# Two banks for x1, a rewritten first chunk border, and x turned into three banks

## The reference

```python
e = stack([tbl_f[ids[:, f]] for f in range(39)], axis=1)      # (512, 39, 16)
x1 = einsum('bid,bjd,ijh->bhd', e, e, W0.reshape(39, 39, 128))
x2 = einsum('bid,bjd,ijh->bhd', e, x1, W1.reshape(39, 128, 128))
z = sum(concatenate([x1, x2], axis=1), axis=-1)               # (512, 256)
h = concatenate([z, dense_ctx], axis=1)
h = maximum(h @ W_top1 + b_top1, 0)                           # 512
h = maximum(h @ W_top2 + b_top2, 0)                           # 256
y = h @ W_top3                                                # (512, 1)
```

## Time and profile before

| what | value |
|---|---|
| median of three runs | 247.56 us (246.15 to 249.37) |
| profiled execution | 246.15 us, span 244.3 us |
| granted TensorE clock, mean | 0.978 of full |
| TensorE matmul busy | 218.0 us (89%) |
| VectorE busy | 160.3 us (66%) |
| ScalarE busy | 156.5 us (64%) |
| GpSimd busy | 119.0 us (49%) |

### The profile page before, as it was taken

The page is one execution under the profiler, slowest core; times in us unless marked ns, Lnnn a source line. Parts: engine busy times, 40 slices in busy tenths (PEclk is TensorE's granted clock), DMA queues, the critical chain, the costliest instruction groups (busy, mean ns, idle before and its releaser), DMA issues.

```text
span 244.3 us, 4536 instructions
## 1 busy us (share of the span) xinstructions
PE 218.0 (89%) x1601; PEld 170.7 (70%) x1601; DVE 160.3 (66%) x325; ACT 156.5 (64%) x300; POOL 119.0 (49%) x119
## 2 busy tenths in 40 slices
PE   4587997999298999979999999998899999999896
PEld 4487565676165677867678588886586788887895
DVE  3988899699339894567686775584868664743101
ACT  3986887779368756466856857577757755653101
POOL 4787788777877877787877878400000000000000
PEclk9959999999979999999999999999999999999999
DMA  5970089030000000000000000000000000000000
GB/s 142 246 251 16 11 241 276 12 91 5 5 7 9 7 10 6 7 7 8 7 7 10 7 7 9 5 0 3 0 0 4 1 0 3 0 0 3 0 3 0
DMA packets 8362, 8.72 MB, mean 36 GB/s; under 512 B 3095, under 2 KB 5948, under 8 KB 8340
## 3 DMA queue, kind: packets, MB, share of 16 engines
q1 hardware_dynamic: 4660, 7.48, 10.8%
q0 software_dynamic: 3680, 0.95, 3.6%
HBM read 8.42 MB, written 0.00 MB: 34 GB/s over the span
## 4 chain that ended last, share of the span: by engine, by line
PE 44%; POOL 32%; issue 14%; ACT 7%; DMA 2%; DVE 1%; ACTq 0%; DVEq 0%
POOL emb L392 32%; PE turn_bank L496 12%; PE x_bank L435 5%; PE pair_bank L417 5%; PE x_bank L438 4%; PE x_bank L437 4%; PE g_bank L474 4%; PE turn_bank L534 3%; PE turn_bank L507 2%; ACT prod_hi L946 2%; PE x_turn_bank L452 2%; ACT prod L941 1%; ACT x1h L958 1%; DMA emb<-tbl,ids_sb 1%; DMA ids_sb<-ids 1%
## 5 line engine op out<-in xcount | busy, mean ns | idle before, releaser
L392 POOL DMA_INDIRECT emb<-tbl,ids_sb x115 | 118.8, 1033 | 37.3 <-issue 34.8
L941 ACT ACTIVATE prod<-pair_bank 128x512 f32<-128x512 f32 (+1 forms) x112 | 65.8, 600 | 46.8 <-PE pair_bank L417 42.0
L435 PE MATMUL x_bank<-prod_hi,pair_w_hi 128*128 128x512 f32 (+1 forms) x112 | 62.5, 558 | 7.4 <-ACT x1h L958 5.9
L787 DVE TENSOR_TENSOR prod_lo<-prod,prod_hi 128x512 fp32r<-128x512 f32 x96 | 64.8, 685 | 2.3
L417 PE MATMUL pair_bank<-x,sel 117*128 117x512 bf16 (+1 forms) x112 | 42.6, 384 | 2.2 <-ACT prod L941 1.5
L496 PE MATMUL turn_bank<-g_sb,w_sb 128*128 128x128 f32 x312 | 42.7, 279 | 0.6 <-ACT g_sb L968 0.6
L496 PEld LDWEIGHTS turn_bank<-g_sb,w_sb 128*128 128x128 f32 x312 | 39.4, 191 | 4.4 <-issue 1.9
L946 ACT ACTIVATE prod_hi<-prod 128x512 fp32r<-128x512 f32 x64 | 40.1, 627 | 0.0
L438 PE MATMUL x_bank<-prod_hi,pair_w_lo 128*128 128x512 f32 x96 | 38.1, 397 | 0.0
L437 PE MATMUL x_bank<-prod_lo,pair_w_hi 128*128 128x512 f32 x96 | 38.1, 397 | 0.0
L777 DVE CAST prod_hi<-prod 128x512 fp32r<-128x512 f32 x48 | 20.5, 428 | 19.7 <-ACT prod L941 19.4
(11 more groups left out here) (138 smaller groups left out, 231.7 us busy)
## 6 DMA issues: line engine op xcount, KB each, us to landing
emb<-tbl,ids_sb POOLq DMA_INDIRECT x115, 2.3
tab<-small SPq DMA_DIRECT2D x2, 560.0 KB
wt<-w_top SPq DMA_DIRECT2D x2, 512.0 KB
tab<-small SPq DMA_DIRECT2D x1, 504.0 KB
wa<-pair_w_a SPq DMA_DIRECT2D x1, 448.0 KB, 5.4
wb<-pair_w_b SPq DMA_DIRECT2D x1, 448.0 KB, 6.2
wtd<-w_dense SPq DMA_DIRECT2D x1, 256.0 KB, 6.9
dense_sb<-dense_t SPq DMA_DIRECT2D x1, 256.0 KB, 7.5
```

The costliest lines, as they stand in the source:

```text
L392: pool.indirect_dma_start(out=emb[:, at:at + D], out_offset=None, in_=tables[f], in_offset=bass.IndirectOffsetOnAxis(ap=ids_sb[:, c * M + ...
L435: mm = pe.matmul(x1_bank[:, :], pair_w_hi[p, t, :], hi(n), start=(t == 0), stop=(t == FULL))
L787: dve.tensor_tensor(lo(n), prod[rows, n % RING, :], prod_hi[rows, n % RING2, :], ALU.subtract).then_inc(lo_done, 1)
L941: act.activation(prod[0:ROWS[t], n % RING, :], pair_bank[n % 2][0:ROWS[t], :], ACT.Square).then_inc(sq_done, 1)
```

## The change

- The two banks `x1_bank` and `x1_turn_bank` become `x1_banks[0]` and `[1]`. Block `k` sums its x1 in bank `k % 2` and turns it in the same bank once it is copied out. The first product of a block waits for `x1_t` of the block before the last, no longer for the copy to `x1h`. The look-ups of the next chunk go to the bank that is free and start one step sooner (last step of blocks 0 and 1 of a chunk).
- x is turned in three parts, slices 0 to 4, 5 to 10 and 11 to 15: into `x1_banks[0]` (chunk 0: `turn_bank`), `misc_bank` and `pair_bank[0]`. VectorE copies the first and third part, ScalarE the second.
- Chunk 2 becomes late as well: `LATE = (1, 2, 3)`.
- At the first border, `SEAM`, a function of its own (`seam`) orders TensorE's work, and VectorE and ScalarE follow: all of chunk 0's `layer1`, its last x1 turning and contractions and its 39 `layer2` products are done around the turning of x and the first four pair products of chunk 1. In blocks 4 to 7 these are left out.

```diff
-LATE = (1, 3)
+LATE = (1, 2, 3)
+TURNS = ((0, 5), (5, 11), (11, 16))
+SEAM = 1
...
+        def later_bank(part):
+            return x1_banks[(part + 1) % 2]
+        def turned_x1(k):
+            return x1_banks[0 if k == K - 1 else k % 2]
+        def turn_banks(c):
+            return (x1_banks[0], misc_bank, pair_bank[0]) if c else (turn_bank, misc_bank, pair_bank[0])
...
             def layer1(n):
                 pe.wait_ge(lo_done, n + 1)
                 if t == 0:
-                    wait(pe, x1_kept, k)
+                    wait(pe, x1_done, k - 1)
+                    c, j = divmod(k, NB)
+                    if j in (1, 2) and c + 1 < NCH and LOOKED[c + 1]:
+                        pe.wait_ge(picked, picks(c + 1, j - 1))
...
             def turn_x1(k):
                 pe.wait_ge(x1_kept, k + 1)
-                wait(pe, x1_done, k)
...
+            def seam(c):
+                n, k = c * NB * NT, c * NB
+                for m in range(n - LAG1, n):
+                    layer1(m)
+                    if m % NT in G_AT:
+                        contract_d(k - 2, G_AT.index(m % NT))
+                turn_x1(k - 1)
+                contract_d(k - 1, 0)
+                turn(c, 0)
+                pe.wait_ge(xblk_done, k)
+                turn(c, 1)
+                pe.wait_ge(sq_done, n - 1)
+                turn(c, 2)
+                contract_d(k - 1, 1)
+                layer2(c - 1, 0, 3)
+                select_pair(n)
+                select_pair(n + 1)
+                turn_x(k)
+                layer2(c - 1, 3, 15)
+                select_pair(n + 2)
+                layer2(c - 1, 15, 27)
+                select_pair(n + 3)
+                layer2(c - 1, 27, M)
...
                 if late and t == 0:
                     layer1(m)
                     layer1(m + 1)
+                    pe.wait_ge(x1_done, n // NT - 1)
+                    turn(c, 0)
+                    pe.wait_ge(xblk_done, n // NT)
+                    turn(c, 1)
                     pe.wait_ge(sq_done, n - 1)
-                    turn(c, 0, pair_bank[n % 2])
-                    pe.wait_ge(xblk_done, n // NT)
-                    turn(c, 1, misc_bank)
+                    turn(c, 2)
                     layer1(m + 2)
...
+                if c + 1 < NCH and LOOKED[c + 1]:
+                    if j in (0, 1) and t == NT - 1:
+                        wait(pe, x1_done, n // NT)
+                        look_up_later(c + 1, j, 0, 2)
+                    if j in (1, 2) and t < 2:
+                        look_up_later(c + 1, j - 1, 2 * t + 2, min(2 * t + 4, HOT))
-                if j == 2 and c >= 1:
+                if j == 2 and c >= 1 and c != SEAM:
                     layer2(c - 1, 3 * t, 3 * t + 3)
...
         def _(dve):
-            def keep_turned(c, to):
-                dve.wait_ge(turned, 2 * c + 1)
...
+            def keep_turned(c):
+                for part in (0, 2):
+                    dve.wait_ge(turned, len(TURNS) * c + part + 1)
+                    dve.tensor_copy(*turned_x(c, part)).then_inc(x3_a, 1)
...
                 if late and t == 6:
                     take_lo(n - 1)
+                    if c + 1 == SEAM:
+                        take_lo(n)
+                        keep_g(k - 1, 0)
+                        keep_g(k - 1, 1)
                     split_rest(c + 1, END)
                     split_lo(c + 1, END)
+                    if c + 1 == SEAM:
+                        keep_g(k, 0)
...
         def _(act):
                 if c in LATE and j == 0 and t == 0:
                     keep_turned(c)
+                    if c == SEAM:
+                        keep_g(k - 1, 1)
                 tile(n)
...
                 if late and t == 6:
+                    if c + 1 == SEAM:
+                        round_hi(n)
+                        keep_g(k - 1, 0)
+                        keep_x1h(k)
+                        keep_g(k - 1, 1)
+                        keep_x1(k)
                     split_first(c + 1, END)
                     split_second(c + 1, END)
+                    if c + 1 == SEAM:
+                        keep_g(k, 0)
```

More of the change, by code:

```diff
@@ L333, in g_out @@
             if k == K - 1 and pair == 1:
-                return x1_turn_bank[:, 0:2 * QC] if half else turn_bank[:, 512 - 2 * QC:512]
+                return turned_x1(k)[:, 0:2 * QC] if half else turn_bank[:, 512 - 2 * QC:512]
             return g_bank[half][:, 0:2 * QC]
@@ L398, in _, with turn @@
         def _(pe):
-            def turn(c, half, to):
+            def turn(c, part):
                 pe.wait_ge(split_first_done, pieces(c))
@@ L403, in turn @@
                 pe.wait_ge(split_done, pieces(c))
-                out = to[0:P3, :].bitcast(BF16).rearrange("p (d b) -> p d b", b=CH)
-                for d in range(D // 2):
-                    mm = pe.transpose(out[:, d, :], parts[:, half * D // 2 + d, :, :].rearrange("b q i -> b (q i)"),
-                                      idb[:, :])
+                d0, d1 = TURNS[part]
+                out = turn_banks(c)[part][0:P3, :].bitcast(BF16).rearrange("p (d b) -> p d b", b=CH)
+                for d in range(d0, d1):
+                    mm = pe.transpose(out[:, d - d0, :], parts[:, d, :, :].rearrange("b q i -> b (q i)"), idb[:, :])
                 mm.then_inc(turned, 1)
@@ L451, in turn_x1 @@
                         pe.wait_ge(x1_kept, K + 1)
-                    mm = pe.transpose(x1_turn_bank[:, g * H:(g + 1) * H], x1h[:, g * 128:(g + 1) * 128], idf[:, :])
+                    mm = pe.transpose(turned_x1(k)[:, g * H:(g + 1) * H], x1h[:, g * 128:(g + 1) * 128], idf[:, :])
                 mm.then_inc(x1_turned, 1)
@@ L553, in step @@
                 k, u = divmod(m, NT)
+                if c == SEAM and j == 0 and t < LAG1:
+                    if t == 0:
+                        seam(c)
+                    return
                 late = c in LATE and j == 0
@@ L643, in _ @@
             pe.wait_ge(picked, len(SETS))
-            turn(0, 0, turn_bank)
-            turn(0, 1, misc_bank)
+            for part in range(len(TURNS)):
+                turn(0, part)
             pe.wait_ge(dense_in, 32)
@@ L792, in tile @@
                     round_hi(n - 1)
-                if LAG <= n < TILES + LAG and not (n % (NT * NB) == 0 and n // (NT * NB) in LATE):
+                if LAG <= n < TILES + LAG and not (n % (NT * NB) == 0 and n // (NT * NB) in LATE or n == NT * NB * SEAM + 1):
                     take_lo(n - LAG)
@@ L832, in step @@
                 looks = c + 1 < NCH and LOOKED[c + 1]
+                seam = c == SEAM and j == 0
                 if c in LATE and j == 0 and t == 0:
-                    keep_turned(c, pair_bank[n % 2])
+                    keep_turned(c)
+                    if seam:
+                        keep_g(k - 1, 1)
                 if t == 1 and splits:
@@ L840, in step @@
                     spread_x(k)
-                if t == 4 and splits:
-                    keep_turned(c + 1, misc_bank)
-                if t == 1 and k >= 2:
+                if t == 1 and k >= 2 and k - NB * SEAM not in (0, 1):
                     keep_g(k - 2, 0)
-                if t == 4 and k >= 2:
+                if t == 4 and k >= 2 and k - NB * SEAM not in (0, 1):
                     keep_g(k - 2, 1)
@@ L848, in step @@
                     later_one_hot(c + 1, j, t - 2)
-                if looks and j in (1, 2) and t == 3:
+                if looks and j in (1, 2) and t == 2:
                     pick_later(c + 1, j - 1)
@@ L950, in tile @@
                     square(n)
-                if n >= 1 and (n - 1) % NT not in DVE_ROUNDS:
+                if n >= 1 and (n - 1) % NT not in DVE_ROUNDS and n != NT * NB * SEAM:
                     round_hi(n - 1)
```

90 lines of the change are left out of this document (38 added, 52 removed).

## The result

The changed kernel takes **237.47 us** (median of four runs, 237.06 to 238.85) against 247.25 us for the kernel before (median of four, 246.15 to 249.37). The ratio is 0.9611, interval 0.9563 to 0.9658: 3.9% faster. The forecast was 241.0 us with a range down to 238.0: right in direction, but the gain was larger than the whole range allowed.

What follows compares the result with a forecast made beforehand. VectorE and TensorE were taken to pace chunk 0, with gather waits at the borders; 3.6 (chunk 2 starting sooner) + 1.1 + 1.5 + 0.4 = 6.6 us off the median of 247.56 gave 241.0 us, range 238.0 to 246.0.

Steps and rivals of the forecast that it cites:

- block 7 and border 2: Block 7 as block 3 (9.0), then 3.65 from last pair product to turning and 1.79 to chunk 2's first pair product.
- gain in chunk 2 with border 3: 1.1 us from three x1 products already done at chunk 2's start, half of the two banks' 1.5, and 0.4 at border 3.
- (d): Two x1 banks remove waits before first x1 products in chunks 2 and 3: 1.5 us (0 to 2.0); nothing in chunk 0.
- the third bank: At borders 2 and 3, turning x in three parts cuts turning to first pair product from 2.24 to 1.79, saving 0.45.
- VectorE and TensorE pace chunk 0 together: Reading of chunk 0: VectorE is busy 8.61 of 9.00 us in block 1 and 8.53 of 8.98 in block 3.
- the gathers cover it: In chunk 0 the two x1 banks gain nothing, since the wait for gathers at border 1 covers it.
- VectorE takes over: Rival: blocks 5 to 7 all take 9.84, losing 2.1 us; gain 4.5, 243.1 us; chance 0.18.
- The clock at the seam: Rival: idle pieces between 62.8 and 67.4 bring TensorE to 1.2 GHz, 2.5 us more; 243.5 us; chance 0.13.
- The rule on transposes: From the Trainium skill: transposes do not count as busy for the clock as products do; would make the seam's low clock likelier.
- The clock low through layer 2: Rival: the clock stays low through 36 layer-2 products after border 1; 10.8 us lost, 251.8 us; chance 0.07.
- Two banks that move the wait: Rival: waits only move to the turning of x1, block 5 loses 0.4, third bank gains nothing; 243.8 us; chance 0.10.
- the wait for x_t: New wait of the look-up late in block 5, with block 6's first pair product queued behind: 0 to 0.5 us.

Runs made afterwards that it cites:

- experiment 4: The changed kernel with x turned in slices of 7, 8 and 1 instead of 5, 6 and 5; 238.31 us, ratio 0.9651 against the kernel before.
- experiment 2: The changed kernel with the old wait for x1h put back before each block's first x1 product, two banks kept; 241.17 us, ratio 0.9807 against the kernel before.
- experiment 3: The kernel before with chunk 2 made late and nothing else changed; 245.63 us, ratio 0.9974 against the kernel before.
- experiment 1: The changed kernel without the seam at border 1, all else kept; 242.27 us, ratio 0.982 against the kernel before.
- experiment 10: The changed kernel with an extra 128x512 VectorE copy in each of the 16 blocks; median 241.04 us, ratio 0.978 against the kernel before.
- experiment 9: The changed kernel with VectorE picking the looked-up rows before it spreads x, in the third step; 238.36 us, ratio 0.9639 against the kernel before.
- experiment 5: The changed kernel with the seam's 39 layer-2 products back in blocks 6 and 7; 384.68 us on a slow chip, repeated on another: 238.88 us, ratio 0.9689.
- 6 (second tries): The changed kernel with look-ups back at their old steps, repeated after a first try on a slow chip; 237.96 us, ratio 0.9678 against the kernel before.
- experiments 7 and 8: The changed kernel without the seam, with 200 extra identity transposes, or 200 identity products, ahead of border 1's turning of x; 245.99 and 246.29 us.

## Why the prediction was wrong

Forecast, by the profiles: a gain of 6.6; measured 8.5. The terms:

| step of the prediction | forecast | measured |
|---|---|---|
| turning of x at border 1 | 67.35 | 66.63 |
| first pair product of chunk 1 | 70.6 | 69.91 |
| its first x1 product | 80.1 to 80.3 | 79.03 |
| block 5 starts | 82.9 | 82.13 |
| block 5, block 6 | 8.9, 9.5 | 8.82, 8.77 |
| block 7 and border 2 | 9.0 - 0.92 + 3.65 + 1.79 = 13.5 | 13.20 |
| chunk 2 starts | 114.8 | 112.92 |
| gain in chunk 2 with border 3: 1.1 + 0.75 + 0.4 | 2.25 | 2.30 |
| gain in chunk 3: other half of (d) | 0.75 | 0.7 |
| turning to first pair product, borders 2 and 3 | 1.79 | 1.74, 1.74 |

**Right.** The direction; the seam as the main source; chunk 2's and chunk 3's gains; the third bank (1.74 against 1.79, and experiment 4 returns 0.4 per border when ScalarE's part is made larger again); no wait for gathers at border 2; the clock at 1.00 through the seam of the profiled run; two x1 banks worth 1.5 in chunks 2 and 3 (experiment 2: 1.4). Experiment 3 confirms that making chunk 2 late is worth about 1.1 in that chunk; and what was gained at its start (5.5 us, 3.6 forecast) came with the seam, for without the seam (experiment 1) it starts where it did.

**Wrong: step (d), which counts the two banks in chunks 2 and 3 alone; "in chunk 0 it is worth nothing", and chunk 1 is given nothing for them.** The whole excess of 1.9 us lies before chunk 2. Experiment 2 sizes it: with the old wait back, chunk 2 starts at 114.89, as forecast (114.8); with the two banks it starts at 112.92. They are worth 1.97 us where the forecast had nothing: 0.58 up to block 5, 1.37 in blocks 5 and 6 and 0.02 behind them. The step rests on the reading that "VectorE and TensorE pace chunk 0 together", since VectorE was busy for 8.61 of 9.00, and the prediction took 8.9 and 9.5 for blocks 5 and 6 on the same ground. With the old wait these blocks take 9.35 and 9.61, without it 8.82 and 8.77: 1.37 us for two waits. And block 2's 9.84, with VectorE busy for only 7.86 of it, had already said that something other than VectorE set its time. Experiment 10 shows VectorE's room directly: 0.42 more work in blocks 5 and 6 costs nothing. VectorE came near to pacing block 1 alone (8.56 of 8.69), and the borders; even in block 1 the order of its pieces, with the same pieces, was worth 0.26 (experiment 9).

**In part wrong, by the same step: "the gathers cover it" at border 1.** With the seam, border 1 has a chain of its own, from the last tile of chunk 0 to the turning (in the profiled run x1h at 63.72, contraction at 65.89). There the gathers were in at 65.70, a wait of 0.56 us on VectorE and none on TensorE's line. So chunk 0's faster blocks do arrive: its last pair product starts at 58.52 with the two banks and at 59.74 with the old wait, and of these 1.22 us 0.58 are left at the turning (66.63 against 67.21) and at block 5 (82.13 against 82.71). But in the profiles of experiments 5, 6 (second tries) and 10, with the same two banks, chunk 0's last pair product starts at 57.73 to 58.05, and there the gathers, in at 66.00 to 66.30, do come last: the turning begins at 66.85 to 67.15, 0.06 to 0.36 ahead of the kernel with the old wait. So chain and gathers end close together, and the cover holds or not by the execution. Of the 0.77 by which block 5 came sooner than forecast the rest, 0.19, is in small terms of the seam, not taken apart.

**Mis-sized: block 7 and border 2**, 13.5 against 13.20. Two errors cancelled in part: block 7 up to its last pair product is 7.34, not 8.1, and from there to chunk 2 it is 5.86, not 5.44. Experiment 2 shows that the two are one quantity (block 7 longer by 0.71, the sum the same), and in experiment 10, with more work for VectorE, the sum grows by 0.45, all of it behind the last pair product: ScalarE's and VectorE's work on the last tiles and the splits sets it.

**The absolute time.** The sum was put against the median of three runs, 247.56, since the profiled run was the lowest of three. The later runs of the kernel before had medians of 246.32 to 246.6, close to the profiled run's 246.15, and the changed kernel's profiled run (237.63) is at its median. So of the 3.5 us between 241.0 and 237.47, 1.9 is mechanism and 1.6 the base that was chosen. From 246.15 the same sum gives 239.5, which is still 1.9 above the changed kernel's profiled run.

**The rivals.** *VectorE takes over* (9.84 in blocks 5 to 7) did not happen, and experiment 10 excludes it for blocks 5 and 6. *The clock at the seam* did not happen in the profiled run, but it did in experiment 5, whose seam is the same up to the turning and had it at 1.2 GHz, and not in experiments 6 and 10 with idle pieces as long or longer. The rule on transposes that was set beside this rival did not hold in experiments 7 and 8. *The clock low through layer 2* came in no profile: in experiment 5, the one seam with a low clock, it was back between 70 and 71. In experiment 1 the low level lasted for some 5.6 us after work was taken up (66.81 to between 72 and 73), longer than the 3 us read from the earlier trace rows, so its chance was not far-fetched. *Two banks that move the wait*: a part of it is real, though not by the wait for x_t that was named, which has no row in block 5. The new wait for the picked rows has 0.8 and 0.9 us in its rows, and in blocks 1 and 5 the gain of the banks is the smaller for it (0.5 against 0.84 in block 6). Experiment 9 puts its price at 0.26 and 0.39.

## What to carry to other kernels

A wait's price is the distance from start to start with and without it, not its idle row: a row of 0.48 us cost 0.71 where the next product would have overlapped the one before it, and a row of 0.90 cost 0.39 where another wait stood behind it. An engine that is busy for 95% of a block is no proof that it paces that block: compare a neighbouring block in which it is busy for less and which still takes as long (block 2 here), before work is counted off against it. And "hidden by the gathers" was read from the schedule of before: when the change itself fills that wait, each gain ahead of it has to be counted again (here 0.06 to 0.58 us of 1.2 got through, by the execution). Last, a stretch in which the granted clock changes differs between two profiles by the clock alone (0.54 us in block 4 in experiment 3): compare the clock rows first.

## What the runs showed of the hardware that was not expected

- Transposes with an identity kept TensorE's granted clock at 1.00 for 11.34 us just as products of the same shape did, at the same speed (200 in 11.34 us each).
- In experiment 1 TensorE's last product before the idle stretch started at 60.96 and took 0.40; the granted clock was already 0.58 in mean from 62 to 63. In experiment 5 it fell although the longest idle piece between 62 and 67.15 was 0.94 us; in experiment 10 it stayed at 1.00 through one of 1.13. In the kernel before it stayed at 1.00 until past 66, with TensorE idle from 62.8. Idle time before the fall alone doesn't tell when it falls.
- One chip ran TensorE's look-up products before block 0 so slowly that the kernel before took 387.23 us and the changed variants 383 to 385, with a mean granted clock of 0.795; the profile names no releaser for the idle time between them. What made it so is open; from block 4 on the two variants took there what they take on the other chip (168.0 us to the end against 168.2 in experiment 5, 165.3 against 165.5 in experiment 6).
